# A two-layer graph network: `W0` times the attention vectors `a` as summed VectorE operations, and the last product's eviction behind the first exponentials

## The reference, cut to what matters

```python
h = jnp.maximum(_layernorm(x, axis=-1), 0.0)          # x: (1250, 512)
h = h @ W + b_w                                       # W: (512, 512)
s_dst = h @ a[:512]
s_src = h @ a[512:]
e = leaky_relu(s_dst[dst] + s_src[src] + b_a, 0.2)
w = exp(e)
denom = segment_sum(w, dst, N)
out = segment_sum((w / denom[dst])[:, None] * h[src], dst, N)
x = x + out
```

## Time and profile before

| | |
|---|---|
| runs of the kernel | 816.26, 819.63, 821.10 us; median 819.63 |
| the profiled execution | 820.28 us; span of its instructions 818.4 us |
| busy, share of the span | PE 95%, PEld 78%, DVE 48%, ACT 34%, POOL 15% |
| mean granted TensorE clock | 0.97 of 2.4 GHz |

### The profile page before, as it was taken

One profiled execution on the slowest core, in us unless ns is written; L12 is line 12 of the kernel. 1 busy time (PEld: TensorE's weight loads), 2 busy tenths in 40 slices (PEclk: granted clock), 3 DMA queues, 4 the chain that ended last, 5 costly groups with the idle time before them and its releaser, 6 DMA issues.

```text
span 818.4 us, 11864 instructions
## 1 busy us (share of the span) xinstructions
PE 774.6 (95%) x3811; PEld 634.9 (78%) x3811; DVE 390.9 (48%) x960; ACT 277.6 (34%) x567; POOL 120.4 (15%) x138
## 2 busy tenths in 40 slices
PE   4979998999899999989999999799999999999994
PEld 2678886888688888767777777688888888888883
DVE  6658887888662257722633334422232332332320
ACT  6746655565633240411422222111221221211210
POOL 4000000000000010750000000223313313313211
PEclk9769998999989999999999999999999999999998
DMA  4100000222231065898996952599637974349900
GB/s 134 53 1 4 4 2 1 74 82 92 90 98 53 2 187 199 261 278 293 320 327 223 354 189 73 157 273 309 191 104 184 303 247 115 71 129 266 339 11 5
DMA packets 46612, 124.77 MB, mean 152 GB/s; under 512 B 7315, under 2 KB 7447, under 8 KB 46537
## 3 DMA queue, kind: packets, MB, share of 16 engines
q1 hardware_dynamic: 27375, 78.40, 29.3%
q0 software_dynamic: 9360, 26.18, 12.8%
q10 hardware_dynamic: 9802, 19.19, 7.1%
HBM read 71.43 MB, written 53.20 MB: 152 GB/s over the span
## 4 chain that ended last, share of the span: by engine, by line
PE 90%; DMA 4%; ACT 3%; issue 1%; DVE 1%; ACTq 0%; POOL 0%; SPq 0%; POOLq 0%; DVEq 0%
PE ps L1510 17%; PE ps L1511 16%; PE ps L1512 16%; PE ps L1897 6%; PE ps L1896 6%; PE ps L1598 3%; PE ps L1824 3%; PE ps L1762 3%; PE ps L1763 3%; DMA raw<-in_L_gnn_Wr 2%; PE ps L1531 2%; PE ps L1655 1%; PE ps L1686 1%; PE ps L1868 1%; PE ps L1907 1%
## 5 line engine op out<-in xcount | busy, mean ns | idle before, releaser
L1897 PE MATMUL ps<-slots,CTs 125*128 x230 | 91.0, 396 | 0.0
L1896 PE MATMUL ps<-slots,CTs 125*128 x207 | 81.5, 394 | 0.0
L1438 DVE CAST CTs<-ps 125x512 fp32r<-125x512 f32 (+1 forms) x69 | 37.4, 596 | 86.2 <-PE ps L1824 86.2
L903 ACT ACTIVATE slots<-he_t 125x512 fp32r<-125x512 f32 x40 | 25.3, 635 | 131.4 <-DVE he_t L1345 123.5
L1345 DVE TENSOR_TENSOR he_t<-ps,b_b 125x512 f32<-125x512 f32 x40 | 27.5, 691 | 81.3 <-PE ps L1512 71.7
L1510 PE MATMUL ps<-W,h2T_hi 128*125 128x512 f32 x160 | 63.8, 399 | 2.2 <-DVE W L1313 2.2
L1483 DVE TENSOR_TENSOR tm<-ps,b_b 128x512 f32<-128x512 f32 x23 | 15.9, 692 | 103.3 <-PE ps L1512 103.3
L641 POOL DMA_INDIRECT out<-tg,rec x23 | 36.8, 1602 | 192.5 <-ACT tg L953 167.8
L1510 PE MATMUL ps<-W,agT_hi 128*125 128x512 f32 x160 | 63.6, 397 | 0.0
L1511 PE MATMUL ps<-W,h2T_hi 128*125 128x512 f32 x160 | 63.5, 397 | 0.0
L1512 PE MATMUL ps<-W,agT_lo 128*125 128x512 f32 x160 | 63.4, 396 | 0.0
(11 more groups left out here) (300 smaller groups left out, 1770.4 us busy)
## 6 DMA issues: line engine op xcount, KB each, us to landing
he_d<-slots SPq DMA_DIRECT2D x30, 448.0 KB
slots<-he_d SPq DMA_DIRECT2D x30, 448.0 KB
w_d<-slots SPq DMA_DIRECT2D x3, 4096.0 KB, 15.7
slots<-w_d SPq DMA_DIRECT2D x24, 512.0 KB, 23.9
t_d<-he_t SPq DMA_DIRECT2D x40, 224.0 KB
c_d<-c_nat SPq DMA_DIRECT2D x10, 546.9 KB
raw<-in_L_gnn_Wl ACTq DMA_DIRECT2D x4, 1024.0 KB, 6.2
raw<-in_L_gnn_Wr ACTq DMA_DIRECT2D x4, 1024.0 KB, 14.1
```

Of the source, the lines that this page charges most:

```text
L903: a.activation(HE[:, t, 0:D], he_t[:, (x * T + t) % 4, :], ACT.Relu).then_inc(he_hi_ready.sem, 1)
L1438: v.tensor_copy(CTs[:, 4 * r:4 * r + n, :], ps[0:P, r, 0:n * S].rearrange("p (c n) -> p c n", n=S)).then_inc(cts_ready.sem, 1)
L1896: mm(o, CTs[:, t, :], part(k, P, t * 1024, P), start=False, stop=False)
L1897: last = mm(o, CTs[:, t, :], part(k, P, t * 1024 + D, P), start=False, stop=t == T - 1)
```

## The change

Part one. `W0` is no longer turned. GpSimd's queue loads `a` to all 128 partitions (`a_b`, 512 KB of writes) and `b_w` to 125 (`bw_b`, 250 KB) in place of `a_c`, `bw_c` and `bw_f`. VectorE multiplies each 128-row chunk of `W0` with a half of `a` and sums along the row (`source_vectors`, `accum_out`): four operations of 128 x 512 for the first half of `a` ahead of the edge tables, four for the second half and two of 125 x 512 for `b_w` behind them. The transposes, the small matmuls, VectorE's four copies and GpSimd's products go. Part two. `product_high(T - 1)` moves on ScalarE behind the second exponentials and the first `p_hi`; `product_low(T - 1)` and the last diagonals (`spread_out(2)`) move on VectorE behind the first `p_lo`.

```diff
-            pool.dma_start(a_c[:], a_vec.rearrange("(w k j) -> k w j", w=2, j=KC)).then_inc(small_in.sem, 16)
-            pool.dma_start(bw_c[:], b_w.rearrange("(k j) -> k j", j=KC)).then_inc(small_in.sem, 16)
+            pool.dma_start(a_b[:].rearrange("p w d -> p (w d)"), a_vec.partition_broadcast(128)).then_inc(small_in.sem, 16)
+            pool.dma_start(bw_b[:], b_w.partition_broadcast(P)).then_inc(small_in.sem, 16)
             pool.dma_start(ba_c[:], b_a.partition_broadcast(P)).then_inc(small_in.sem, 16)
-            pool.dma_start(bw_f[:], b_w.unsqueeze(0)).then_inc(small_in.sem, 16)
...
-            pool.wait_ge(*small_in(64))
-            link(g.tensor_tensor(ab_c[:], a_c[:, 0, :], a_c[:, 1, :], ALU.add))
-            g.tensor_tensor(ab_c[:], ab_c[:], bw_c[:], ALU.mult).then_inc(ab_ready.sem, 1)
...
             row_out(0)
-            product_high(T - 1)
...
                 if 1 <= g <= NP * QN:
                     weights_high(g - 1)
+                if g == 1:
+                    product_high(T - 1)
...
+            def source_vectors(w):
+
+                for c in range(KC):
+                    if w * KC + c >= 2:
+                        dve.wait_ge(*wa_f_ready(w * KC + c - 1))
+                    v.scalar_tensor_tensor(spill[c % 2][:], W0_f[:, c, :], 1.0, a_b[:, w, :], ALU.mult, ALU.mult,
+                                           accum_out=wa_f[:, c, w:w + 1]).then_inc(wa_f_ready.sem, 1)
+
+            dve.wait_ge(*w0_in(16))
+            dve.wait_ge(*small_in(48))
+            source_vectors(0)
             dve.wait_ge(*spans_spread(1))
...
-            for j in range(KC):
-                dve.wait_ge(*w0_turned(j + 1))
-                v.tensor_copy(W0_t[:, j, :], ps[:, 4 + j % 2, :]).then_inc(w0t_ready.sem, 1)
+            source_vectors(1)
+            for w in range(2):
+                dve.wait_ge(*wa_f_ready(2 * KC - 1 + w))
+                v.scalar_tensor_tensor(spill[w][0:P, :], bw_b[:], 1.0, a_b[0:P, w, :], ALU.mult, ALU.mult,
+                                       accum_out=ab[:, w:w + 1]).then_inc(ab_ready.sem, 1)
...
-                if g == 1:
-                    product_low(T - 1)
-                    dve.wait_ge(*sd_spread(1))
-                    spread_out(2)
                 if 1 <= g <= NP * QN:
                     weights(g - 1)
...
+                if g == 2:
+                    product_low(T - 1)
+                    dve.wait_ge(*sd_spread(1))
+                    spread_out(2)
...
-                if 8 <= u < 8 + KC:
-                    if u == 8:
-                        pe.wait_ge(*w0_in(16))
-                    turn_w0(u - 8)
-                if u == 16:
-                    pe.wait_ge(*small_in(64))
-                    pe.wait_ge(*w0t_ready(KC))
-                if 16 <= u < 16 + KC:
-                    wa_part(u - 16)
-                if u == NU - 2:
-                    pe.wait_ge(*ab_ready(1))
-                    for c in range(KC):
-                        last = mm(ps[0:P, 4, 0:1], ones[:, 0:P], ab_c[:, c:c + 1], start=c == 0, stop=c == KC - 1)
-                    last.then_inc(ab_summed.sem, 1)
```

More of the change, by code:

```diff
@@ L147, in gnn_kernel @@
         q_sel = at("q_sel", [2 * CR + 1, CR, P], F32R, R1 + 20480)
-        W0_t = at("W0_t", [128, KC, D], F32, R1)
+        a_b = at("a_b", [128, 2, D], F32, R1)
+        bw_b = at("bw_b", [P, D], F32, R1 + 4096)
+        spill = [at(f"spill_{k}", [128, D], F32, R1 + 6144 + 2048 * k) for k in range(2)]
         g_b = at("g_b", [NW, NCH], F32, 28704)
@@ L189, in gnn_kernel @@
         fl_f = early("fl_f", [1, 2], F32)
-        a_c = early("a_c", [128, 2, KC], F32)
-        bw_c = early("bw_c", [128, KC], F32)
-        ab_c = early("ab_c", [128, KC], F32)
+        wa_f = early("wa_f", [128, KC, 2], F32)
+        ab = early("ab", [P, 2], F32)
         wa = early("wa", [128, KC, 4], F32R)
@@ L197, in gnn_kernel @@
         spark = early("spark", [1, 1], F32)
-        bw_f = early("bw_f", [1, D], F32)
         bw_2 = early("bw_2", [33, D], F32R)
@@ L343, in gnn_kernel @@
         step_used, window_out = signals("step_used window_out", BW)
-        (w0_hi_ready, w0_lo_ready, w0_turned, w0t_ready, wa_done, wa_ready, ab_ready, ab_summed,
+        (w0_hi_ready, w0_lo_ready, wa_f_ready, ab_ready, wa_ready,
          var_ready, std_ready, norm_ready, h_ready, turned, hT_hi_ready, hT_lo_ready, s_done, hw_done,
          hw_hi_ready, hw_lo_ready, bw_hi_ready, bw_lo_ready, sums_used, small_ready, s_ready, sd_ready, sd_spread, row_ready) = signals(
-             "w0_hi_ready w0_lo_ready w0_turned w0t_ready wa_done wa_ready ab_ready ab_summed "
+             "w0_hi_ready w0_lo_ready wa_f_ready ab_ready wa_ready "
              "var_ready std_ready norm_ready h_ready turned hT_hi_ready hT_lo_ready s_done hw_done "
@@ L746, in _ @@
                 if u == 10:
-                    act.wait_ge(*small_in(64))
+                    act.wait_ge(*small_in(48))
                     act.wait_ge(*small_ready(1))
-                    copy(bw_2[0:1, :], bw_f[:]).then_inc(bw_hi_ready.sem, 1)
+                    copy(bw_2[0:1, :], bw_b[0:1, :]).then_inc(bw_hi_ready.sem, 1)
                 if u == 12:
@@ L1065, in _ @@
             dve.wait_ge(*bw_hi_ready(1))
[L1066 to L1072, removed]
+            v.tensor_tensor(bw_2[32:33, :], bw_b[0:1, :], f32(bw_2[0:1, :]), ALU.subtract).then_inc(bw_lo_ready.sem, 1)
+            dve.wait_ge(*wa_f_ready(2 * KC))
+            link(v.tensor_copy(wa[:, :, 0:2], wa_f[:]))
+            v.tensor_tensor(wa[:, :, 2:4], wa_f[:], f32(wa[:, :, 0:2]), ALU.subtract).then_inc(wa_ready.sem, 1)
+            dve.wait_ge(*ab_ready(2))
+            v.tensor_scalar(s_add[:], ab[:, 0:1], ab[:, 1:2], ba_c[:], ALU.add, ALU.add).then_inc(wa_ready.sem, 1)
             dve.wait_ge(*std_ready(1))
@@ L1533, in hot_block @@
                 last.then_inc(hot_made.sem, 1)
[L1535 to L1544, removed]
-                for c in range(KC):
-                    last = nc.tensor.transpose(ps[:, 4 + j % 2, c * 128:(c + 1) * 128],
-                                               W0_f[:, c, :].rearrange("p (k j) -> p j k", j=KC)[:, j, :], ident[:])
-                last.then_inc(w0_turned.sem, 1)
             def spread_spans():
```

## The result

The changed kernel takes 809.49 us (median of 13 runs, 808.34 to 815.44) against 818.79 us for the kernel before (13 runs, 815.96 to 822.27): a ratio of 0.9905, 95% interval 0.9883 to 0.9927, so faster by some 0.95%, or 9.3 us (6.0 to 9.6 by the interval). The prediction was 811 in a range of 806 to 816, with 0.87 on faster. The execution that was profiled took 812.0 us (span 810.1), 8.3 us less than the one before.

A forecast was written before the change was run, and what follows sets the result against it. TensorE, 90% of the chain of waits, was taken to bound the kernel. The profiled 820.28 us less 4.9 (part one) and 4.0 (part two) gave 811.4, or 810.7 against the median, stated as 811; range 806 to 816.

The forecast's parts named there:

- The mark: Start of ScalarE's L719 (first `h_f`) ahead of the chunk loop: from 47.9 to 43.0 us, 4.9 us gained.
- L: Landing time of the new loads that VectorE's first sum waits for: 16.5 us taken, between 14.0 and 17.4.
- D: Delay of VectorE's edge tables past TensorE's asking near 21 us: 2.0 us, shifting ScalarE's line by as much.
- t: Duration of one VectorE operation with a sum: 0.61 to 0.80 us, 0.70 taken.
- VectorE's own line: VectorE's path from the landing of `x` through statistics to shift: ends 39.9 to 43.3 us, under or at ScalarE's.
- the prediction's late case: New loads share the busy DMA engines with `x`: 3.4 us added, L = 17.4, second half of `x` landing at 32.4.
- Half rate: Rival, chance 0.12: VectorE's summed operations run at half rate, t = 1.17, gain at the mark 2.5 us, total 813.8.
- Whatever moves it moves everything: At L719, 47.91 us: a gain there was taken to pass to the kernel's end in full.
- Part two: Attention's start: standstill 1.3 us, clock holds, second matmul group at 133.75 instead of 137.75 us, 4.0 us gained.
- The rival in which the clock falls: TensorE's clock falls in the shorter standstill before attention: gain there 2.3 us, total 813.1; chance 0.22.
- From 151 us to the end: After 151 us TensorE is nearly always busy, so earlier gains were taken to reach the end in full.
- the 8.9 forecast: Whole kernel: 4.9 us from the mark and 4.0 us from attention's start, both taken off the profiled time.

The follow-up runs named there:

- Experiments 4 and 5: 4: changed kernel, each half of `x` loaded as 112 and 13 rows (cuts), 809.75 us; 5: changed kernel, edge tables ahead of the first four sums, 808.93 us.
- Experiment 7: Changed kernel plus 13 matmuls into an unused bank ahead of the loop's first pass, 812.73 us; the same with `x` cuts and tables first, 808.02 us.
- experiment 3: Kernel before plus 12 matmuls, written to a bank nobody reads, in TensorE's standstill at 129 us: 816.35 us (0.9971 to before).
- experiment 6: Changed kernel with `x` loaded in 112 and 13 rows and tables ahead of the first sums, run on two occasions: 807.04 us (0.9848) and 809.23 us (0.9907).
- part two alone: Kernel before with only `product_high(T - 1)` and `product_low(T - 1)` moved as in the change: 815.25 us (0.9950 to before).
- the one with a single filler in experiment 8: Changed kernel with `x` cuts and tables first, plus 14 matmuls in TensorE's wait for `nat_lo` near 217 us: 809.52 us (0.9890 to before).
- the kernel before with the cuts: Kernel before with `x` loaded in cuts of 112 and 13 rows, nothing else: 818.68 us (0.9992 to before).

## Why the prediction was right

**The mark** was put at 43.0 and came at 43.80, a gain of 4.1 and not 4.9. Each input was near: L 16.75 (16.5 taken), D 1.86 (2.0), and t 0.61 (0.70). What failed is "VectorE's own line ... under or at ScalarE's". The prediction gave that line 39.9 to 43.3, as `x` lands at 29 to 32.4, and kept ScalarE as the one that decides. `x` landed at 32.87, past the late end, and VectorE's line ended there too, at 43.80. Experiments 4 and 5 show it from both sides: with `x` early the mark moves, with the tables early it does not. D, the term that carried the working, cost nothing. The number survived, by luck as much as by working, since the two lines end only 1.0 us apart: ScalarE's gives 42.80 where it decides (experiment 4).

Two things moved `x`. The traffic ends 3.1 us later (the last packet of 2048 bytes, the size of `x`'s, at 32.4 for 29.3), near the 3.4 of the prediction's late case. And the landing that VectorE sees comes 0.5 us behind the end of the traffic (32.87 for 32.4), which the 29 and the 32.4 of the prediction leave out. All that was added is the two broadcasts. Their packets, which the trace has one by one, show that they share engines with `x`: on eleven engines both are through by 11.2 us, on five they go on in rounds of five packets to 15.2 us. They also show that `bw_b` was not split over five engines, as the prediction took it, but over all 16: it goes in 62 packets of 4096 bytes and a single one of half that, as sixteen shares of eight rows (the last of five) give; five shares of 25 rows would leave five halves. At the prediction's 24 GB/s the late case is then 48 KB per engine, an estimate of 2.0 us; where the other 1.1 of the 3.1 come from is not shown.

**Half rate** is ruled out: an operation with a sum pitches at 0.61 us for 512 columns, as one without a sum does (0.59 for 500), and reading the accumulator takes 0.08 us under the next operation. The Trainium skill's rule (*Vector Engine (DVE) Microarchitecture Reference*, "Points that are easy to get wrong"), by which this would be 1.17, does not hold here: the measurement decides.

**A term that was missing:** the loop's first pass. "Whatever moves it moves everything" was wrong by 1.1 us in these two profiles, and by some 0.7 in the mean of all of them. Of 4.12 us at the first turning of `h_f`, 3.04 reach the first product with `W0_hi`. With `W0` no longer turned and multiplied, TensorE works 6.84 us between 35 and 48 where it worked 12.35. It stands 3.50 us ahead of its last block of one-hots, and makes the four turnings and the 25 counts of the pass at 1.2 GHz (5.33 us for the 25); before, with the same turnings at 1.07 us, the clock rose within the counts (4.26 us). Experiment 7 takes this loss away.

**Part two** was put at 4.0; it is 3.8 in the changed kernel and 3.8 alone. The standstill is 1.40 (1.3), the clock holds, and the second twelve products start 3.42 us behind the first (3.45), with the wait of 0.41 us for `p_lo` that the working has too. The rival in which the clock falls did not come. That the clock is worth more than half of it is shown by experiment 3, where only the clock was changed. This part came by the forecast's own mechanism.

**From 151 us to the end** the gain was to pass in full: 6.9 at `p_sum`, 6.9 at the turning of `crow`. This pair agrees (365.27 and 365.25 us from one to the other), but the 14 profiles of all versions have 362.6 to 368.9 us for this stretch, and one and the same program in experiment 6 has 368.9 and 365.1. One pair of profiles therefore can't show that a gain passes. The 1.5 us behind it are the granted clock after TensorE's wait for `crow`, about 2 us long in both. In windows of 13 and 11.5 us from there (before, then after):

```profile
517.00:530.00 13.00, 11.60 (x55) 9.83 (x56) 5.32 (x9) 1.32 (x2) 2.85 (x3) 0.88 0.29 89
```

```profile
510.00:521.50 11.50, 10.03 (x55) 8.38 (x55) 5.22 (x9) 1.32 (x2) 2.87 (x3) 1.00 0.34 107
```

And the ten transpositions that end the wait, before and after:

```profile
516.77 2.46 PE L1824 MATMUL ps<-ident,crow 128*125 128x128 f32 x10 [2.05 <-DMA crow<-c_d,rec]
```

```profile
509.85 1.33 PE L1802 MATMUL ps<-ident,crow 128*125 128x128 f32 x10 [2.11 <-DMA crow<-c_d,rec]
```

The version with the cuts waited 2.08 us there, and its clock fell as before's did (0.87 over 508 to 521); of the other versions' profiles none fell there, but four did behind the next waits, for `hrow` and `heT`, 1.2 to 1.4 us long in nearly all: part two alone (0.88 over 518 to 532), the tables first, the version with cuts, tables and matmuls, and the one with a single filler in experiment 8. From the turning of `hrow` to the end these four took 290.1 to 290.4 us, the others 288.8 to 289.0. Waits of the same length came out either way, so I count this 1.5 us as chance of one profile and not as the change's. Without it the profile gives 6.9 us against the 8.9 forecast: the sum of both parts was 2.0 too high (0.8 at the mark, 1.1 in the first pass, 0.2 in part two).

**The total** is nearer than its terms, and that is in part luck. The medians lie 9.3 us apart, 2.4 more than the profiles account for, and where these come from stays open; single runs of the changed kernel spread over 7 us, and the interval of 6.0 to 9.6 us holds the 6.9 of the profiles as well as the 8.9 of the forecast.

## What to carry to other kernels

- When two engines' lines end close together, forecast the later of the two, and ask of each what its last input is. Here the transfer that the new loads push back was listed, but the line behind it was left below the other one.
- Taking work from TensorE ahead of a phase can cost clock in that phase (some 0.7 us here). Count the first pass at the lower level until a row shows otherwise, and look at every standstill: cutting one from 3.5 to 1.4 us gave 3.8 us, and 2.4 could be had with idle matmuls alone.
- What is won at one start need not show in the time: gains of 2.7 and 2.4 us past the changed kernel's at 142 us gave a better ratio on one occasion and the same one on the other. Compare the kernels at several places, not only at the end, and take two profiles of one program before a difference of 1 us is given a cause.

## What the runs showed of the hardware

- Landing times of transfers that count up one semaphore can't be read one by one: the view gives `a_b` 6.8 us from its issue, while its last packets end 9.1 us behind it.
- A load of 125 rows keeps a share of 0.33 of the DMA engines; cut into 112 and 13 rows its traffic ends by 20 us where it took until 32.4, and 228 GB/s flow from 0 to 20 us instead of 156. GpSimd's queue beside it is through at 15.9 us instead of 15.7.
- The record of the granted clock reads 1.00 throughout 35 to 48 us in the changed kernel, while its one-hot matmuls last as long as before's, beside which it reads 0.50: four of L1538 from 35.38 take 2.08 us, and four of before's L1531 from 33.66 take 2.08. In the first 55 us the durations of matmuls tell the level, not the record.
- The standstill of 1.4 us before attention left the clock at 1.00 in every version that had it; those of 3.5 us there and of 4.4 us at `nat_lo` were followed by 0.50 in every version that left them empty. When it falls differs: at 131 us in before, 2 us into the standstill, and at 134 in the kernel before with the cuts, whose first five products behind the same standstill still start every 0.23 us. The standstills of 1.9 to 2.1 us before `crow`, and the shorter ones at `hrow` and `heT`, came out both ways.
